# Attention up to its turned result in the experts stage instead of the combining stage

## The reference

```python
# attention: q, k, v = x @ w_qkv.T, 16 heads of 16
q = elu(q) + 1
k = elu(k) + 1
kv = einsum('bnhd,bnhm->bhdm', k, v)
z = 1.0 / (einsum('bnhd,bhd->bnh', q, k.sum(axis=1)) + 1e-06)
out = einsum('bnhd,bhdm,bnh->bnhm', q, kv, z)
attended = out.reshape(b, n, d) @ w_out.T + b_out
# experts: each token goes to the 2 best of 16 experts; for each expert
s = silu(x @ W1.T + b1) * (x @ W3.T + b3)      # 127 wide
h = concat([sqrt(sum(s * s) + 1), s])          # 128 wide
o = h @ W2.T + b2                              # 255 wide
row = concat([sqrt(sum(o * o) + 1), o])
# the two rows of a token and a shared one are combined with two norms
```

## Time and profile before

| | |
|---|---|
| median of 3 runs | 1770.83 us (1770.51 to 1777.24) |
| span of the profiled execution | 1773.8 us |
| experts stage, first projection to the first issue of the next stage | 377.95 to 609.78 us |
| combining stage, first issue to last store's issue | 609.78 to 923.42 us |
| busy over the whole span: PE, DVE, ACT, POOL | 77%, 78%, 71%, 69% |
| mean granted clock of TensorE: experts stage, combining stage | 1.00 (400 to 600 us), 0.74 (700 to 800 us) |

### The profile page before, as it was taken

One profiled execution on the slowest core, in us unless ns is written; L12 is line 12 of the kernel. 1 busy time (PEld: TensorE's weight loads), 2 busy tenths in 40 slices (PEclk: granted clock), 3 DMA queues, 4 the chain that ended last, 5 costly groups with the idle time before them and its releaser, 6 DMA issues. The chain is left out here.

```text
span 1773.8 us, 63284 instructions
## 1 busy us (share of the span) xinstructions
PE 1368.2 (77%) x21833; PEld 947.5 (53%) x21834; DVE 1388.7 (78%) x3576; ACT 1252.4 (71%) x3382; POOL 1218.6 (69%) x1312
## 2 busy tenths in 40 slices
PE   3549999969899736455534899999997799999857
PEld 2515555545555425344422566666664566666646
DVE  7878877856566479988846999999984688888748
ACT  7818888846666568778837888888753677777745
POOL 6738888733233488777615899999974677787747
PEclk9999999989999977777767999999998999999969
DMA  8627787769999657766643566665643122222239
GB/s 259 226 94 183 206 198 196 198 156 211 206 219 220 183 158 177 199 162 169 167 113 89 115 125 128 126 129 118 123 102 77 45 53 53 52 52 52 53 97 290
DMA packets 495359, 256.31 MB, mean 145 GB/s; under 512 B 359357, under 2 KB 484864, under 8 KB 494720
## 3 DMA queue, kind: packets, MB, share of 16 engines
q1 hardware_dynamic: 482658, 219.11, 51.0%
q0 software_dynamic: 12576, 35.67, 6.7%
HBM read 79.52 MB, written 73.44 MB: 86 GB/s over the span
## 5 line engine op out<-in xcount | busy, mean ns | idle before, releaser
L213 PE MATMUL ps<-all_late,l_xq_T 128*128 128x352 f16 x1536 | 252.5, 316 | 57.3 <-DMA l_xq_T<-l_apart 30.7
L213 PEld LDWEIGHTS ps<-all_late,l_xq_T 128*128 (+1 forms) x1536 | 146.9, 99 | 149.4 <-DVE ffn_h L711 45.9
L213 PE MATMUL ps<-l0moe_W,all_xT_all 128*128 128x16 f16 (+2 forms) x1152 | 190.6, 312 | 32.0 <-ACT all_xT_all L912 22.3
L1455 POOL TENSOR_TENSOR all_late<-experts_se,all_mhalf 128x4 f32<-128x4 f32 (+1 forms) x77 | 76.4, 993 | 159.9 <-DVE experts_se L1564 145.4
L2308 POOL TENSOR_TENSOR all_late<-ret_pm,all_late 128x512 f16<-128x512 f32 x128 | 145.5, 1158 | 20.8 <-ACT all_late L2214 20.8
L213 PEld LDWEIGHTS ps<-l0moe_W,all_xT_all 128*128 128x128 f16 x1152 | 83.6, 100 | 117.0 <-ACT all_xT_all L912 26.0
L619 PE MATMUL ps<-all_late,ffn_hT 128*128 128x256 f16 x1088 | 131.9, 276 | 9.3 <-ACT l_xq_T L683 5.8
L1720 PE MATMUL ps<-l_kvm,both_q 128*128 128x136 f16 x384 | 38.3, 269 | 122.5 <-DVE both_o L1893 112.1
L213 PE MATMUL ps<-moe_E,experts_gT 128*128 x864 | 117.4, 276 | 15.4 <-DMA experts_gT<-slots_dram 10.6
L619 PEld LDWEIGHTS ps<-all_late,ffn_hT 128*128 128x128 f16 x1088 | 106.8, 99 | 29.8 <-issue 8.0
L364 POOL TENSOR_TENSOR ffn_h<-ffn_fq_val,ffn_h 128x704 f16<-128x704 f32 x64 | 97.5, 1523 | 14.9 <-ACT ffn_h L359 14.9
(11 more groups left out here) (301 smaller groups left out, 4697.2 us busy)
## 6 DMA issues: line engine op xcount, KB each, us to landing
rows_dram<-all_late SPq DMA_DIRECT2D x72, 256.0 KB
ret_v<-ret_vpad SPq DMA_DIRECT2D x256, 64.0 KB
front_xin<-x SPq DMA_DIRECT2D x16, 512.0 KB, 4.3
x_dram<-front_x SPq DMA_DIRECT2D x16, 512.0 KB, 5.0
all_late<-x_dram SPq DMA_DIRECT2D x64, 128.0 KB
z_dram<-all_late SPq DMA_DIRECT2D x64, 128.0 KB
both_zin<-z_dram SPq DMA_DIRECT2D x16, 512.0 KB
both_xin<-x SPq DMA_DIRECT2D x16, 512.0 KB
```

The lines of the kernel that those rows point to most:

```text
L213: mm = pe.matmul(out, lhs[a], rhs[b], start=first and n == 0, stop=last and n == 2, skip_group_check=True)
L1455: pool.tensor_tensor(rows[:, n % 4, which, :, 0], se[:, u, which], power[:, which], ALU.pow).then_inc(s_time, 1)
```

## The change

The attention of a pair of token tiles, from the query matmuls to the DMA transpose of its result, leaves the combining stage for the experts stage. What is turned goes over the token tiles in `xT_all`, whose pair has been read by the query matmuls. The projection with `w_out` stays in the combining stage and reads all of it from there. A pair p is done in the steps of tiles 2p and on; there are 32 pairs and 72 tiles of experts. The engines get these skews, counted from tile 2p: TensorE queries 0, numerators 5; ScalarE negative 1, query_hi 3, attended_hi 8; VectorE query 2, query_lo 3, divide 6; GpSimd the low part behind power step 2p+8; SyncE the transpose in its step 2p+10. Buffers are moved: the float32 ones lie in the weights `W` and in `kv_sum`, which are no longer needed, and PSUM banks 0, 1, 6 and 7 are used, with the down block's outputs in 4 and 5.

```diff
-def phase_experts(nc, ps, E16, ..., blocks, heads):
+def phase_experts(nc, ps, E16, ..., blocks, heads,
+                  xT_all, wq, spare):
...
-            unrolled(count, [(7, turn_hidden), (0, turn_rows), (11, store)])
+            def turn_attended(t):
+                p = t.n // 2
+                if t.n < TILES and t.n % 2 == 0:
+                    sp.wait_ge(s_ohi, p + LAG + 1)
+                    sp.wait_ge(s_olo, p + LAG + 1)
+                    sp.dma_start_transpose(xT_all[:, t.n:t.n + U].rearrange("p k c m -> p (k c) m"),
+                                           o16[:, p % LAG].rearrange("p k a d -> p (k a d)")).then_inc(s_oT[p % LAG], 16)
+            unrolled(count, [(7, turn_hidden), (0, turn_rows), (11, store), (10, turn_attended)])
...
+            def attended_lo(p):
+                pool.wait_ge(s_ohi, p + LAG + 1)
+                pool.tensor_tensor(o16[:, p % LAG, :, 1], o[:, p % LAG], o16[:, p % LAG, :, 0], ALU.subtract).then_inc(s_olo, 1)
...
             for n in range(count + OLAG):
                 times(n)
+                if n % 2 == 0 and 0 <= n - 8 < TILES:
+                    attended_lo((n - 8) // 2)
...
-            pipeline(pe, count, [(EXPERT_LAG, experts_both), (0, experts_first), (EXPERT_LAG, down), (0, project)], 12)
+            scheduled(pe, [(EXPERT_LAG, count, experts_both), (0, count, experts_first), (EXPERT_LAG, count, down),
+                           (0, TILES, queries), (5, TILES, each_pair(numerators)), (0, count, project)], 12, 12, 4)
...
-            pipeline(act, count, [(7, output), (3, hidden_hi), (1, gate)], 4)
+            scheduled(act, [(7, count, output), (3, count, hidden_hi), (1, count, gate), (3, TILES, each_pair(query_hi)),
+                            (8, TILES, each_pair(attended_hi)), (1, TILES, each_pair(negative))], 4, 12, 13)
...
+            scheduled(dve, [(7, count, out_clamp),
+                            (2, count, square),
+                            (2, count, hidden_clamp),
+                            (2, TILES, each_pair(query)),
+                            (3, count, hidden_lo),
+                            (1, count, hidden),
+                            (3, TILES, each_pair(query_lo)),
+                            (6, TILES, each_pair(divide))], 4, 12, 13)
...
 (combining stage)
-            stages = [(8, output), (4, numerators), (0, queries)]
+            stages = [(6, output)]
-                attend(2 * i, [(7, turn)])
-                attend(2 * i, [(7, out_lo)])
-            upper = [(6, out_hi), (3, query_hi)]
-            stages = [(2, query), (5, divide), (3, query_lo)]
```

More of the change, by code:

```diff
@@ L146, in pipeline, with scheduled, step @@
         step(None, s)
+def scheduled(eng, stages, slots, first, passes):
+    def step(c, i=None):
+        for skew, count, stage in stages:
+            k = c - skew
+            if i is not None:
+                stage(Tile(slots * i + k, k % LAG, slots // LAG * i + k // LAG, k % slots))
+            elif 0 <= k < count:
+                stage(Tile(k, k % LAG, k // LAG, k % slots))
+    for c in range(first):
+        step(c)
+    with eng.Fori(0, passes) as i:
+        for r in range(slots):
+            step(first + r, i)
+    for c in range(first + slots * passes, max(skew + count for skew, count, _ in stages)):
+        step(c)
 def unrolled(count, stages, slots=LAG):
@@ L160, in pair_of, with each_pair, run @@
     return Tile(t.n // 2, t.slot4 // 2, t.n // 4)
+def each_pair(stage):
+    def run(t):
+        if t.slot4 % 2 == 0:
+            stage(Tile(t.n // 2, t.slot4 // 2 % LAG, t.n // 4))
+    return run
 def even(stage):
@@ L1406, in phase_experts @@
         hp = [ps[:, 2 + u, 0:U * up].rearrange("p (k n) -> p k n", k=U) for u in range(LAG)]
[L1407 removed]
+        op = [ps[:, 4 + u, 0:U * OUTW].rearrange("p (k n) -> p k n", k=U) for u in range(LAG)]
         block = ph.enter_context(nc.Block())
@@ L1506, in down, with queries @@
                 ins.then_inc(s_down, 1)
-            pipeline(pe, count, [(EXPERT_LAG, experts_both), (0, experts_first), (EXPERT_LAG, down), (0, project)], 12)
+            def queries(t):
+                if t.slot4 % 2 == 0:
+                    p = Tile(t.n // 2, t.slot4 // 2 % LAG, t.n // 4)
+                    x = xT_all[:, bass.ds(t.n, U)]
+                    pe.wait_ge(s_qp, free(p))
+                    for j in range(C):
+                        for c in range(C):
+                            w = [wq("q", c, part, j * P, P) for part in range(2)]
+                            for n, (a, b) in enumerate(((0, 0), (1, 0), (0, 1))):
+                                ins = pe.matmul(qps[p.slot][:, j], w[a], x[:, :, b * C + c], start=c == 0 and n == 0 and j == 0,
+                                                stop=c == C - 1 and n == 2, skip_group_check=True)
+                    ins.then_inc(s_q, 1)
@@ new lines, in numerators @@
+            def numerators(p):
+                if isinstance(p.n, int) and p.n == 0:
+                    pe.wait_ge(s_step, BATCH * C + 2)
+                pe.wait_ge(s_qlo, done(p))
+                pe.wait_ge(s_qhi, done(p))
+                pe.wait_ge(s_o, prev(p))
+                for k in range(U):
+                    for c in range(C):
+                        kv = [kvm16[:, bass.ds(p.n // (TB // U), 1), part, c].rearrange("p o k -> p (o k)")
+                              for part in range(2)]
+                        for n, (a, b) in enumerate(((0, 0), (1, 0), (0, 1))):
+                            ins = pe.matmul(nps[:, k, c], q16[:, p.slot, a, c, k * P:(k + 1) * P], kv[b],
+                                            start=c == 0 and n == 0, stop=n == 2, skip_group_check=True)
+                ins.then_inc(s_num, 1)
@@ L1698, in _ @@
         def _(pe):
[L1699 to L1722, removed]
+            prime(pe, s_out)
             def output(t):
-                pe.wait_ge(s_oT[t.slot], landed(t))
                 if t.n >= OUTS:
```

174 lines of the change are left out of this document (78 added, 96 removed).

## The result

The changed kernel takes 2033.16 us (median of 4 runs, 2031.42 to 2035.27) against 1773.67 us of the kernel before in the same comparison. The ratio is 1.147, with a 95% interval of 1.144 to 1.150. The prediction was 2115 us with a range of 2025 to 2165: slower as forecast, by 260 us where 341 were forecast. The profiled execution has a span of 2033.5 us, 259.7 more than before.

The account below looks back on a forecast made before the run. It took a circle of waits through SyncE's order to bound the experts stage at 19.06 us per two tiles: 1773.8 (span) + 414 (experts) - 70 (combining) = 2118, less 3.0 to the median, so 2115 us, range 2025 to 2165.

Parts of the forecast that it names:

- The circle: Experts stage: down block, output, power step, low part, attended turn, hidden turn wait on each other; 19.06 us per two tiles.
- the 7.3 us in the earlier trace: Kernel before: SyncE issued tile 41's hidden turn 7.3 us before GpSimd ended the powers of tile 45.
- ScalarE's extra: Experts stage: ScalarE's steps between projection and output take 2.4 us where TensorE's way is 1.25, so 1.15 more.
- the landing: Hidden turn's issue to TensorE's release: 3.87 us, with 1.24 us of delay behind the pair's data; bounds 2.7 and 5.2.
- the half-clock share: TensorE after some 8 us idle runs at clock 0.50: down block 2.1 us, queries 2.76 + 0.15 us.
- The number of rounds: Experts stage: first attended turn issued at 412.0, then 31 rounds of 19.06 us to the last at 1002.9.
- The combining stage: GpSimd's gathers and power step set 13 rounds of 13.6 us; stage 244 us, 70 us less than before.
- The circle at full clock: Rival, chance 0.13: TensorE's bursts get clock 1.00 after 8 us idle; circle 16.7 us, whole 2042 us.
- The harmless place on SyncE: Rival, chance 0.04: the attended turn's place costs nothing and TensorE's 8.2 us per two tiles bound; 1775 us.
- the faster one: Rival, chance 0.03: place harmless and TensorE's new work fills its own gaps; two tiles 7.5 us, whole 1752 us.
- Table loads: ScalarE, Exp beside Tanh in the experts stage: charged zero; two loads per pair would add some 2.6 us to the circle.

Follow-up runs that it names:

- The runs with the place repaired: Changed kernel with attended turn in step 2p+14 or 2p+12, low part behind power step 2p+6, or that plus turn in 2p+11: 1755.02, 1755.10, 1753.80, 1742.78 us.
- the run with 12: Changed kernel with SyncE's turn of an attended pair in step 2p+12 instead of 2p+10: 1755.10 us, ratio 0.990 to the kernel before.
- the run with 66: Changed kernel with 66 more TensorE matmuls for each pair, behind the projection of the odd step: 2009.68 us, ratio 1.131 to the kernel before.

## Why the prediction was right, and by how much it was off

**The circle.** Shown, from three sides: by taking it out through SyncE (278 us less), by taking it out through GpSimd with SyncE as it was (279 us less), and by putting it alone into the kernel before (189 us more). The point that decided the forecast, that the hidden turn of tile s-6 stands behind a wait for power step s-2, came from the order in the diff and one number, the 7.3 us in the earlier trace rows.

**Its size.** 17.15 us measured against 19.06:

| term | predicted | measured |
|---|---|---|
| hidden turn's issue to TensorE | 3.87 | 2.71 |
| down block, queries (mostly half clock) | 5.01 | 4.23 |
| projection | 1.76 | 1.83 |
| down(s-5) to the output, with ScalarE's extra | 2.40 | 2.28 |
| output to the end of the power step | 3.40 | 3.55 |
| low part | 1.24 | 1.22 |
| attended turn | 1.40 | 1.33 |

The term that failed is the landing. The step said that the pair's data go ahead of the hidden turn's and hold it up by 1.24 us, worked out from one row of the combining stage. The hidden turn landed 2.71 us after its issue, as without a pair ahead of it (2.69). The pair was through by then. From the list of issues from 500 to 860 us, with the median us from issue to landing (3.2 to 3.3 in all 21):

```profile
all_xT_all<-experts_o SPq DMA_TRANSPOSE x21, 3.3
```

That is 0.6 us more than a hidden turn, not 1.24, and the hidden turn, issued 1.33 us later, landed 0.7 us behind it. Of the 3.93 us of the earlier trace rows, 0.44 lie in the issue, which took 1.68 us there and 1.24 here; I had put them and the rest down to size. The lower bound, 2.7, was the true value: 36 us of the whole. The Trainium skill's 261 GB/s (DMA: Bandwidth & Descriptors, "Latency and other measured facts") gave 36 us less because by it the pair would be through in time, and in this the run agrees with the page against my reading of the row; it does not measure that rate.

The second is the half-clock share, 0.78 us too large. The clock came back 4.9 us after the burst began, as expected, but the down block took 1.67 us to the queries, not 2.1, and the queries 2.56 to the projection, not 2.91. The 1.17 us of the down block hold a gap of some 0.3 us: without it the block takes 0.87 us at full clock in the same round (585.02 to 585.89). I had doubled the gap too and taken it off once, and had added a gap to the queries where the next matmuls start ahead of the end of the last. That is 24 us over the stage.

**The number of rounds.** I let 31 rounds cost the same. The first 27 took 17.08 us on average, the last four 14.8: from tile 64 on there are no queries, and their 2.6 us leave the circle. This was to be read from the diff. The first attended turn went out at 403.8 instead of 412.0. The added matmuls ahead of it cost 4.3 us (23.6 us from power step 0 to power step 8, 19.3 before) where I took 7. The larger part is chance: power step 0 itself came at 377.99 instead of 383.34, since SyncE had issued the stage's first row turns at 367.97 instead of 373.34, ahead of anything that the change touches in this stage. In the runs with the same start of the stage it came between 377.2 and 383.0. Rounds and start are 17 us of the 84.

**The combining stage.** 234.6 us against 244. The rounds were right, 13.4 to 14.0 behind a first one of 12.2 against 13.6, and so was GpSimd as their bound. The four rounds without gathers had been taken at 10, 10, 10 and 6; the power steps follow there at 8.4, 8.3 and 5.7 us, so this tail was 8 us shorter. With it the four items come to 86 us, against the 84 that were missed. All of them went the same way, none paid for another, and the measured time lies only 8 us above the lower end of the range.

**The rivals.** The circle at full clock is not what happened (clock 0.70), but its time, 2042 us, lies nearest to the measured one, because other terms were too large. The harmless place on SyncE was priced at 1775 us and the faster one at 1752. The runs with the place repaired took 1743 to 1755: of the 8.2 us that TensorE's work adds up to, only 7.6 to 7.9 were needed, though two tiles had taken 6.17 and not 5.9 on average before. The experts stage ended 42 to 63 us later, where 74 were priced. One reason shows in the rows of the run with 12: a projection and a down block follow there at 2.46 us (545.23 to 547.69) where they took 2.93, because TensorE's small gaps ahead of each are gone. That is what the faster rival said.

**Table loads.** None stands in the experts stage: tanh, the high part, Relu and Exp begin at 585.22, 585.50, 586.02 and 586.64. The profile agrees with zero, and with the set that the Trainium skill names (ScalarE: Activation LUTs, "Table sets: the hidden batching unit").

## What to carry to other kernels

An issue queue that is written out in order has a place in time, not only an order. Before a wait is put on it, ask which instruction the waited one hangs on, and compare it with what stands behind the wait: if that feeds the same chain, it is a circle, and its length is the period, whatever the engines' loads. The move of work to a stage where engines have room was right here and worth 1.0 to 1.7%, but only once the waited instruction no longer hung on that chain. A price read from one row needs its issue and its size taken apart before it is scaled.

## What was not expected of the hardware

With TensorE idle for only 1.98 us, after 5.84 us of matmuls without a gap, the granted clock still fell from 1.00 to 0.50, and did so after the next burst had begun (row 581 is idle at clock 1.00, row 583 is busy at 0.50):

```profile
581.00:582.00 1.00, 0.00 (x0) 0.00 (x0) 0.00 (x0) 0.00 (x0) 0.00 (x0) 1.00 0.65 126
583.00:584.00 1.00, 1.00 (x6) 0.68 (x6) 0.00 (x0) 0.00 (x0) 0.00 (x0) 0.50 0.58 114
```

The next burst, 16 us later in the same run, had 2.20 us of idleness ahead of it and queries of 2.74 us. In the run with 66 the idleness was 0.17 us in one round and 1.09 us in the next (ahead of 598.69), and the queries took 1.48 us in both. And a turn of 256 KB issued 1.3 us ahead of one of 128 KB did not delay the smaller one's landing (2.71 us against 2.69 us without it).
